# One 512-column reciprocal per group of softmax sums instead of two of 256, with all engines' orders drawn up anew

## What is computed

```python
x = x + attn(layernorm(x))        # landmark attention, 64 landmarks
x = x + xattn(layernorm(x), ctx)  # attention to 64 context rows, masked
x = x + ffn(layernorm(x))         # 1 of 8 experts per sequence, by its last row

# attn
sim1 = q @ k_l.T; sim2 = q_l @ k_l.T; sim3 = q_l @ k.T
attn1, attn2, attn3 = softmax(sim1), softmax(sim2), softmax(sim3)
V = attn2
for _ in range(6):
    KV = attn2 @ V
    V = 0.25 * V @ (13 I - KV @ (15 I - KV @ (7 I - KV)))
out = attn1 @ (V @ (attn3 @ v)) @ Wout + bout
```

## Time and profile before

| | us |
|---|---|
| median of 3 runs | 1449.49 |
| lowest, highest run | 1448.49, 1451.19 |
| the profiled execution | 1447.71 |
| its span in the profile | 1446.0 |
| PE busy | 1406.5 (97%) |
| DVE busy | 1024.6 (71%) |
| ACT busy | 668.0 (46%) |
| POOL busy | 569.9 (39%) |

### The profile page before, as it was taken

One profiled execution on the slowest core, in us unless ns is written; L12 is line 12 of the kernel. 1 busy time (PEld: TensorE's weight loads), 2 busy tenths in 40 slices (PEclk: granted clock), 3 DMA queues, 4 the chain that ended last, 5 costly groups with the idle time before them and its releaser, 6 DMA issues.

```text
span 1446.0 us, 54622 instructions
## 1 busy us (share of the span) xinstructions
PE 1406.5 (97%) x24180; PEld 926.0 (64%) x24180; DVE 1024.6 (71%) x2162; ACT 668.0 (46%) x1204; POOL 569.9 (39%) x799
## 2 busy tenths in 40 slices
...
DMA packets 40540, 53.25 MB, mean 37 GB/s; under 512 B 9698, under 2 KB 30450, under 8 KB 40306
## 3 DMA queue, kind: packets, MB, share of 16 engines
...
## 4 chain that ended last, share of the span: by engine, by line
PE 92%; issue 3%; DVE 2%; POOL 1%; ACT 1%; POOLq 0%; DVEq 0%; DMA 0%; SPq 0%; ACTq 0%
PE bank L1225 43%; PE bank L1475 8%; PE bank L1243 7%; PE bank L1253 7%; PE bank L1462 5%; PE bank L1430 2%; PE bank L1371 2%; PE bank L1324 2%; PE bank L1233 2%; PE bank L1303 2%; PE bank L1443 2%; PE bank L1360 2%; PE bank L1338 1%; PE bank L1330 1%; PE bank L1421 1%
## 5 line engine op out<-in xcount | busy, mean ns | idle before, releaser
L691 POOL TENSOR_TENSOR b<-ut,eye 128x256 f32<-128x256 f32 x192 | 136.4, 730 | 297.8 <-DVE ut L1065 271.5
L1225 PE MATMUL bank<-xnT_c,w1e 128*128 128x512 f32 x256 | 124.0, 610 | 1.4 <-DMA b1e<-in_b 1.4
L1225 PE MATMUL bank<-xnT_a,wqkv 128*128 128x512 f32 x256 | 125.3, 613 | 0.0
L1056 DVE SCALAR_TENSOR_TENSOR wb<-bank,eye 128x256 f32<-128x256 f32 x192 | 73.6, 411 | 72.5 <-PE bank L1243 72.5
L1225 PE MATMUL bank<-w2e,hT 128*128 128x256 f32 x512 | 118.3, 384 | 1.3 <-ACT hT L910 1.3
L1121 DVE RECIPROCAL oT_x<-bank 128x256 f32<-128x256 f32 x64 | 107.8, 1724 | 14.2 <-PE bank L1475 14.1
L1121 DVE RECIPROCAL oT<-bank 128x256 f32<-128x256 f32 x64 | 111.7, 1749 | 3.1 <-PE bank L1475 2.9
L1225 PEld LDWEIGHTS bank<-w2e,hT 128*128 128x128 f32 x512 | 94.9, 190 | 17.0 <-issue 2.3
L850 ACT ACTIVATE az<-bank 128x320 f32<-128x320 f32 x192 | 66.8, 400 | 67.9 <-PE bank L1243 63.6
L869 ACT ACTIVATE pT_x<-bank,neg_bias 128x512 f32<-128x512 f32 x128 | 77.9, 688 | 42.1 <-PE bank L1464 42.0
L585 POOL TENSOR_SCALAR var_eps_c<-mv_c 128x2 f32<-128x2 f32 x32 | 7.2, 225 | 223.0 <-DVE mv_c L930 222.8
...
## 6 DMA issues: line engine op xcount, KB each, us to landing
...
```

The lines of the kernel that those rows point to most:

```text
L691: return g.tensor_tensor(b7[:, q, :], ut[:, q, :], eye[28 if it else 7][:].unsqueeze(1) .broadcast_to([P, 4, LM]), ALU.subtract).then_inc( ...
L1056: return v.scalar_tensor_tensor(wb[:, h], src, 1.0 / 16 if it else 1.0, eye[15][:].unsqueeze(1).broadcast_to([P, 4, LM]), ALU.mult, ALU.ad ...
L1225: last = mm(dst, lhsT, rhs, start=(k == 0), stop=(k == len(pairs) - 1))
```

## The change

The two halves of each reciprocal become one instruction of 512 columns, so VectorE issues 64 reciprocals of the sums where it issued 128. The tables `TURN` and `LAST` are new throughout, for all five engines (some 320 words of one and 1000 of the other). The arithmetic is the same. The diff, with the tables cut to two lines:

```diff
 TURN = """
...
-    P.f.1-2 P.s2-3 D.uz.4.0-4 G.b7.5.1-4 G.b7.5.0-4 P.xnTc.0-5 P.iZ.5-4 A.xnTc.0-5 S.w2.5-3 P.iT.5-4
...
+    P.den1.1-2 P.jT.4-2 A.xnTc.0-3 D.rec1.0-2 D.ut.4.0-2 D.ut.4.1-2 P.f.7-1 P.s2-1 P.jZ.4-2 S.f.2-1
+    G.b7.5.0-2 D.uz.4.1-2 D.uz.4.0-2 A.f.7-1 G.b7.5.1-2 S.ew1-3 G.base-3 P.iT.5-2 D.wb.5.1-2 D.wb.5.0-2
...
@@ -218,7 +216,7 @@
         if kind in ("rec1", "recx"):
-            return (("den" + kind[-1], n[0]), (0,)) if n[1] == 1 else None
+            return ("den" + kind[-1], n[0]), (0,)
         if kind == "kx":
             return step, (0, 1)
@@ -1112,18 +1110,16 @@
                 if kind in ("rec1", "recx"):
                     x = kind[-1]
-                    k, part = step[1:]
-                    if c := unmet(dve, "P", i, ("den" + x, k)):
+                    if c := unmet(dve, "P", i, ("den" + x, n)):
                         dve.wait_ge(pe_done, c)
                     if c := unmet(dve, "P", i - 1, ("w" + x, 0), ("w" + x, 1)):
                         dve.wait_ge(pe_done, c)
-                    cols = slice(part * (S // 2), (part + 1) * (S // 2))
-                    return v.reciprocal(oT[x][:, k, cols], tile(i, ("den" + x, k))[:, cols]).then_inc(dve_done, 1)
+                    return v.reciprocal(oT[x][:, n, :], tile(i, ("den" + x, n))[:]).then_inc(dve_done, 1)
                 if kind in ("o1", "ox"):
                     x = kind[-1]
                     if c := unmet(dve, "P", i, step):
                         dve.wait_ge(pe_done, c)
-                    if c := unmet(dve, "D", i, ("rec" + x, n, 0), ("rec" + x, n, 1)):
+                    if c := unmet(dve, "D", i, ("rec" + x, n)):
                         dve.wait_ge(dve_done, c)
```

More of the change, by code:

```diff
@@ L29 @@
 TURN = """
[L30 to L44, removed]
@@ L51 @@
[L51 to L55, removed]
@@ new lines @@
+    A.e1.1.3-2 P.jZ.3-2 D.uz.3.1-2 P.q.1-1 P.logit-3 D.uz.3.0-2 A.e1.1.2-2 G.b7.4.0-2 D.lmq.0-1 P.iT.4-2
+    P.den1.0-2 D.logit-3 A.nmC.0-3 S.out.0-4 P.iZ.4-2 A.q.1-1 A.e1.1.1-2 G.ksq-1 D.wb.4.0-2 D.wb.4.1-2
+    D.lmq.1-1 P.xnTc.0-3 S.f.1-1 A.e1.1.0-2 S.w2.7-1 S.ctx-1 G.qbd-1 P.f.1 A.az.4.0-2 A.az.4.1-2
+    P.den1.1-2 P.jT.4-2 A.xnTc.0-3 D.rec1.0-2 D.ut.4.0-2 D.ut.4.1-2 P.f.7-1 P.s2-1 P.jZ.4-2 S.f.2-1
+    G.b7.5.0-2 D.uz.4.1-2 D.uz.4.0-2 A.f.7-1 G.b7.5.1-2 S.ew1-3 G.base-3 P.iT.5-2 D.wb.5.1-2 D.wb.5.0-2
@@ L62 @@
+    P.iZ.5-2 A.az.5.0-2 P.h.2-3 D.rec1.1-2 D.fb A.az.5.1-2 P.jZ.5-2 P.h.3-3
 """
 LAST = """
[L67 to L86, removed]
@@ L97 @@
[L97 to L102, removed]
@@ L169 @@
-    D.mxx.0.3@15 D.mxx.1.2@15 D.mxx.0.2@15 D.mxx.0.1@15 D.mxx.0.0@15 P.wx.0@14 P.y3.1@13 P.xnTc.1@14
-    D.mpx@15 D.wx.0@14 P.vx@15 D.lnC.0@14 D.vx@15 P.mTx@15 A.xnTc.1@14 G.rsC.0@14 A.mTx@15 P.gate@14
-    D.y3.1@13 P.tx.0@15 A.gate@14 P.tx.1@15 A.ex.0.2@15 S.out.1@13 P.logit@14 D.logit@14 A.ex.1.3@15
-    A.ex.1.1@15 A.ex.1.2@15 A.ex.1.0@15 P.denx.1@15 S.out.0@13 S.ew1@14 S.ew2@14 A.nmC.0@14 P.xnTc.0@14
-    A.ex.0.3@15 D.recx.1.0@15 P.ox.1@15 A.ex.0.1@15 A.xnTc.0@14 G.x1b@15 G.base@14 A.ex.0.0@15
@@ L174 @@
-    P.denx.0@15 D.recx.1.1@15 P.ox.0@15 P.h.0@14 P.h.1@14 A.h.1@14 D.recx.0.0@15 P.h.2@14 D.recx.0.1@15
-    D.ox.1@15 A.h.2@14 A.h.0@14 D.ox.0@15 P.wx.1@15 D.wx.1@15 D.lnC.1@15 P.h.3@14 A.h.3@14 P.wx.0@15
-    G.rsC.1@15 G.row@14 A.nmC.1@15 P.y3.0@14 D.wx.0@15 P.xnTc.1@15 D.lnC.0@15 A.xnTc.1@15 G.rsC.0@15
-    A.nmC.0@15 P.gate@15 A.gate@15 D.y3.0@14 P.logit@15 P.y3.1@14 P.xnTc.0@15 D.logit@15 A.xnTc.0@15
-    D.y3.1@14 S.ew1@15 P.h.2@15 A.h.2@15 P.h.3@15 S.out.1@14 S.ew2@15 S.out.0@14 G.base@15 G.row@15
@@ new lines @@
+    A.nmC.1@11 A.e1.0.2@12 G.b7.3.1@12 A.q.0@13 G.b7.3.0@12 P.xnTc.1@11 D.wx.0@11 A.xnTc.1@11 P.iZ.3@12
+    A.az.3.1@12 A.az.3.0@12 P.iT.3@12 P.gate@11 D.lnC.0@11 D.vx@12 D.wb.3.1@12 P.t1.1@12 A.gate@11
+    D.wb.3.0@12 P.jT.3@12 D.ut.3.0@12 D.ut.3.1@12 A.e1.1.0@12 P.jZ.3@12 P.q.1@13 D.uz.3.0@12 D.uz.3.1@12
+    P.logit@11 G.b7.4.1@12 G.b7.4.0@12 G.rsC.0@11 A.q.1@13 P.iT.4@12 A.e1.1.1@12 P.den1.0@12 D.lmq.0@13
+    P.iZ.4@12 A.nmC.0@11 D.logit@11 A.e1.1.3@12 D.wb.4.0@12 D.lmq.1@13 D.wb.4.1@12 A.az.4.1@12
```

222 lines of the change are left out of this document (133 added, 89 removed).

## The result

| | us |
|---|---|
| kernel before, beside these runs | 1450.34 |
| changed kernel, median of 4 runs | 1486.24 (1484.17 to 1487.34) |
| ratio, 95% interval | 1.0248, 1.0234 to 1.0262 |
| its profiled execution, and its span | 1487.2, 1485.4 |

The direction was as predicted. The size was not: 1471 was forecast, with 1480 as the upper end. Of all runs told of here one, of `late_half`, took 2777 us, far above every other, and is left out of that kernel's ratio; its median of 1481.74 is taken with it, and would be 1480.85 without.

The account below looks back on a forecast made before the run. TensorE's steps back to back were taken to bound the middle turns. Thirteen turns of 1.31 + 0.35 us gave 21.6 on 1447.7, so 1469.3; the median stands 1.8 higher: 1471, range 1460 to 1480.

Parts of the forecast that it names:

- What bounds the kernel: Middle turns: TensorE busy 84.80 of 84.80 us, so VectorE's savings are worth nothing and added TensorE waits are paid in full.
- The reciprocals: VectorE: 64 of 512 columns at 3.35 us replace 128 of 256, saving 9.6 us of its work, worth 0.
- The new wait: In each turn TensorE waits at `iT.5` for the `uz` made of `jZ.4`: 1.31 us, lower bound 1.0.
- Rival (d): No change: TensorE's steps have slack and catch up after the wait, turn stays 84.8, time 1449; chance 0.03.
- The walk's side remark: At `iT.5`: with `jZ.4` 1.1 us earlier, the long reciprocal would still hold `uz` to about 612.9, `iT.5` to about 613.1.
- More changes of shape: TensorE's turn: 56 borders between array shapes instead of 53, adding 0.35 us a turn; bounds 0 and 0.6.
- Turns of the sum: Thirteen batches with the new sequence: 13 x (1.31 + 0.35) = 21.6 us.
- Rival (a): A second wait, of `y` for `uz.5` behind the whole second reciprocal: 0.5 us a turn more, time 1478; chance 0.14.
- ends of -8 and +5: First batches and end of the kernel: 0 net taken, with -8 and +5 us kept as bounds.
- The check I had named: Sign of a wrong size: the turn is over 87 us, or the ends differ by over 5 us.

Follow-up runs that it names:

- late_half: Changed kernel with each reciprocal in two halves again, the second half of the first behind `uz.4`, that of the second behind `uz.5`; `jZ.4` still late: 1481.74 us, ratio 1.0214.
- early_whole: Changed kernel with `s2` and `xnTc.0` moved behind `jZ.4`, as in the old order, reciprocals still whole: 1485.37 us, ratio 1.0254.
- early_half: Changed kernel with `s2` and `xnTc.0` behind `jZ.4` and reciprocals in halves, other new orders kept: 1471.05 us, ratio 1.0148.
- newturn_oldlast: Changed kernel with the old order of the last steps, reciprocals whole and the new order of the repeated turn kept: 1474.63 us, ratio 1.0163.

## Why the prediction was right in mechanism and wrong in size

- **What bounds the kernel.** Right. TensorE's steps back to back set the middle, and 1.2 us of wait in each turn came out in full.
- **The reciprocals.** 3.35 us predicted, 3.35 and 3.33 measured. VectorE's saving is worth 0, as predicted, and is smaller than forecast besides: 6.7 us by the two groups of reciprocals, 0.8 by the engine's busy time, not 9.6.
- **The new wait.** Predicted at `iT.5`, on `uz`, from 1.91 us between the starts of `jZ.4` and `iT.5`; measured 2.00. Right in place, 0.1 us short in size. The 0.60 us that the working takes off for the `jZ` itself stands in no row. The row gives 0.67, and with it the wait would have been 1.24 instead of 1.31; the profile counts 1.21 a turn. Rival (d) calls the idle time of the earlier trace rows 1.2 us where the row has 1.09, which changes nothing. The walk's side remark, that an early `jZ.4` would still leave the wait because `ut.4`, `uz.4` and `b7` stand behind the long reciprocal, is what `early_whole` shows: 86.3 against 86.6.
- **More changes of shape.** The turn grew by 1.85 us, of which 1.2 to 1.4 are the wait, so that some 0.4 to 0.6 us are left where I had 0.35. `early_half`, which has neither long reciprocals nor the late `jZ.4`, keeps 0.7 us over 84.8. That is at or a little above the upper bound of 0.6; whether it is all borders was not separated.
- **Turns of the sum.** 21.6 us forecast, 22.7 measured up to `xnTa.1` of batch 15. That they agree so well is partly luck. The thirteen turns alone gave 24.9, since a turn lost 1.85 us where 1.66 were forecast, and since the last of them took 89.3 us (86.7 in `newturn_oldlast`, so that the new order of the last steps already tells there). The head's gain of 2.1, for which I had put nothing, took most of the excess away.
- **Rival (a)**, a second wait at `y`, did not come: the turn is 86.6, below the 87 that I had named for it.
- **The step that failed** is "for the first batches and for the end, whose orders are also new, I take 0 net", with ends of -8 and +5. The first batches gave -2.1; the end gave **+16.7**. I had written that the end holds "the same work and ... the same kinds of waits". The amount of work was the same. Two things were missing. I walked the queues in the repeated turn only, and not SP's queue in the last steps, where `ew1` of batch 14 had gone from ahead of `ew2` to behind it and a store: TensorE now ran out of other steps 1.4 us after the load was issued, where its first user had come 6.9 us after it. And I priced a wait at its own length. In this stretch the clock went to 1.2 GHz behind such waits, and the matmuls behind them paid as well: 4.6 us of added idle time came with 12.1 us of slower matmuls. My bound of +5 would have held the idle time alone.
- **The check I had named**, "wrong in size if the ends differ by over 5 us", is the one that came true.

With the end's order put back, `newturn_oldlast` took 1474.6, which is 3.6 above the forecast; its last stretch is still 5.6 us longer than before. Of these 5.6 us, 3.0 are idle time of TensorE (20.6 against 17.6) and 2.6 slower matmuls (175.0 against 172.4). That stretch holds rounds of batches 14 and 15 with whole reciprocals; which waits they lengthen was not tried. The other 5 us or so of the new order's cost at the end, beside the load, stay open too.
